# The first chunk of four routed stages is counted and placed directly behind its choice, ahead of the other work of the two engines

## What is computed

```python
for layer in (L0_ffn, L0_attn, L0_ffn, L1_ffn, L1_attn, L1_ffn, L2_ffn, L2_attn, L2_ffn, L3_ffn, L3_attn, L3_ffn):
    x = x + (0.5 if it is an ffn else 1.0) * layer(layernorm(x))

def L1_ffn(x):                      # 16 experts, at most 640 choices each
    probs = softmax(x @ router_w + router_b)
    vals, idx = top_k(probs, 2); vals = vals / (sum(vals) + 1e-9)
    oh_e = one_hot(idx.reshape(-1), 16)
    pos = (cumsum(oh_e, axis=0) * oh_e).sum(axis=1) - 1     # place among the expert's tokens
    within = pos < 640
    y = mlp_of_expert(idx, x) * vals * within               # silu(x @ wg) * (x @ wu) @ wd
    return x + mlp(x, shared weights) + sum over the two choices of y

def L2_ffn(x):                      # 8 experts, no limit
    scores = softmax(x @ gate_w.T); idx = top_k(scores + gate_b, 2)
    return sum over the two choices of scores[idx] * expert(idx, x) + expert(x, shared weights)
```

## Time and profile before

| | us |
|---|---|
| median of 3 runs | 3057.28 |
| the runs | 3051.14 to 3066.15 |
| the profiled execution | 3060.05 |
| its span, first to last instruction | 3058.6 |
| busy: PE, DVE, ACT, POOL | 2527.5, 2111.4, 1805.1, 1184.4 |
| mean granted TensorE clock | 0.908 of full speed |

### The profile page before, as it was taken

The page is one execution under the profiler, slowest core; times in us unless marked ns, Lnnn a source line. Parts: engine busy times, 40 slices in busy tenths (PEclk is TensorE's granted clock), DMA queues, the critical chain, the costliest instruction groups (busy, mean ns, idle before and its releaser), DMA issues.

```text
span 3058.6 us, 67855 instructions
## 1 busy us (share of the span) xinstructions
PE 2527.5 (83%) x25429; PEld 1999.9 (65%) x25429; DVE 2111.4 (69%) x7749; ACT 1805.1 (59%) x3508; POOL 1184.4 (39%) x1634
## 2 busy tenths in 40 slices
PE   7889988759598776669489999999999977784885
PEld 3466665447377554446479999999999865453554
DVE  6667766864377833844588888888888887336876
ACT  5344445424264432446379999999999855452553
POOL 4200003566433656565662222222222236555412
PEclk9799998879798788779799999999999998896997
DMA  9900000014110133235100000000000001441001
GB/s 238 285 13 3 3 3 1 15 60 143 59 46 3 44 116 108 90 100 170 44 24 13 1 14 13 1 13 7 7 14 1 1 1 44 132 141 30 23 3 29
DMA packets 148390, 157.20 MB, mean 51 GB/s; under 512 B 15585, under 2 KB 123746, under 8 KB 148066
## 3 DMA queue, kind: packets, MB, share of 16 engines
q1 hardware_dynamic: 119618, 78.14, 9.6%
q0 software_dynamic: 28448, 74.71, 7.7%
HBM read 77.79 MB, written 75.01 MB: 50 GB/s over the span
## 4 chain that ended last, share of the span: by engine, by line
PE 40%; DVE 10%; POOL 5%; issue 3%; DMA 1%; ACT 1%; POOLq 0%; DVEq 0%; ACTq 0%
PE banks L3244 7%; PE banks L3259 7%; PE banks L3189 3%; POOL bins L2982 3%; PE banks L3225 2%; PE banks L3198 2%; PE banks L3206 2%; PE banks L3224 2%; PE banks L3182 2%; PE banks L3020 1%; PE banks L3021 1%; PE banks L3031 1%; PE banks L3033 1%; PE banks L3022 1%; POOL results L1439 1%
## 5 line engine op out<-in xcount | busy, mean ns | idle before, releaser
L3341 POOL TENSOR_SCALAR shared_floats<-shared_floats 128x2 f32<-128x2 f32 x256 | 57.3, 224 | 658.0 <-DVE shared_floats L3332 657.8
L3259 PE MATMUL banks<-layer,shared_floats 128*128 128x128 f32 x2048 | 291.2, 275 | 0.0
L3259 PEld LDWEIGHTS banks<-layer,shared_floats 128*128 128x128 f32 x2048 | 258.8, 192 | 0.0
L3244 PE MATMUL banks<-shared_floats,layer 128*128 128x256 f32 x1024 | 245.5, 383 | 0.0
L3580 ACT ACTIVATE shared_floats<-banks,layer 128x256 f32<-128x256 f32 x512 | 210.4, 471 | 52.0 <-PE banks L3244 51.9
L3244 PEld LDWEIGHTS banks<-shared_floats,layer 128*128 128x128 f32 x1024 | 187.5, 193 | 20.8
L3343 POOL TENSOR_TENSOR shared_floats<-shared_floats,neg_half 128x2 f32<-128x2 f32 x256 | 183.2, 716 | 21.3
L1359 POOL DMA_INDIRECT results<-shared_floats,e_token_rows x160 | 155.0, 969 | 88.9 <-issue 48.2
L3353 DVE TENSOR_SCALAR shared_floats<-banks,shared_floats 128x128 f32<-128x128 f32 x512 | 185.9, 404 | 4.0 <-POOL shared_floats L3343 4.0
L244 PE MATMUL banks<-ident,xn 128*128 128x128 f32 x320 | 63.6, 332 | 140.8 <-issue 81.7
L2131 DVE TENSOR_REDUCE shared_floats<-banks 128x2 f32<-128x512 f32 (+3 forms) x256 | 110.8, 485 | 95.9 <-PE banks L1995 94.6
(11 more groups left out here) (398 smaller groups left out, 7974.0 us busy)
## 6 DMA issues: line engine op xcount, KB each, us to landing
bins<-zero SPq DMA_DIRECT2D x1, 18176.0 KB, 70.1
bins<-layer SPq DMA_DIRECT2D x16, 650.0 KB, 12.3
shared_floats<-bins SPq DMA_DIRECT2D x32, 325.0 KB, 3.7
expert_weights<-in_dram_experts SPq DMA_DIRECT2D x32, 312.0 KB, 3.0
results<-results SPq DMA_DIRECT2D x32, 256.0 KB, 3.2
layer<-in_dram_layers SPq DMA_DIRECT2D x8, 902.0 KB, 4.5
results<-zero SPq DMA_DIRECT2D x1, 4096.0 KB, 16.1
bins<-xn,f_bin_row POOLq DMA_INDIRECT x256, 2.3
```

What stands on the lines that cost most here:

```text
L3244: m = T.matmul(k.bank[5 + half][:, part], w["w1"][:, tile(n)], h1[:, :], start=True, stop=True)
L3259: m = T.matmul(to, hidden[:, n * S + t * P:n * S + (t + 1) * P], w["w2"][:, tile(n)], start=False, stop=(n == NF - 1), skip_group_check=True)
```

## The change

In `ffn1` on PE, `count(0)` goes ahead of `ln_turn(1)`. On DVE, the clearing of the carried counts goes ahead of `route(0)`; `place(0)` goes directly behind `route(0)`; `apply(1)`, which was inside `route(0)`, goes behind `place(0)`, and so do the two clearings of e_hidden1. In `ffn2` on PE, `widen` is split in its two wide matmuls and the tails (`widen_tails`), and `count(0)` goes between the two, ahead of the tails and of `logits(1)`. On DVE, `place(0)` goes directly behind `route(0)`, ahead of `statistics(2)` (in the run that has it) and of `multiply(0)`. The chunks 1 to 7 keep their order; no instruction is added or taken away; ACT, POOL and SP keep theirs. The lines of the new kernel are up to 9 higher.

```diff
 def ffn1_tensor
     logits(0)
+    count(0)
     ln_turn(k, s, 1)
-    count(0)
     for i in range(NC):
         widen(i)
 def ffn1_vector
-        if i + 1 < NC:
+        if i and i + 1 < NC:
             apply(i + 1)
         top_weights(k, n, 1e-9)
...
     v.count(V.memset(hidden[1][:, :], 0.0))
+    v.count(V.memset(carry[:, :], 0.0))
     route(0)
-    v.count(V.memset(carry[:, :], 0.0))
+    place(0)
+    apply(1)
     for n in range(2):
         v.count(V.memset(k.sb(f"e_hidden1_{n}", [P, CAPACITY])[:, :], 0.0))
-    V.wait_ge(v.sem, v.n)
     for i in range(NC):
         n = s.c0 + i
-        place(i)
+        if i:
+            place(i)
         multiply(i)
 def ffn2_tensor
         m.then_inc(k.sem("f1_gate_up"), 1)
+
+    def widen_tails(i):
+        n, xnT = s.c0 + i, k.xnT(s.t0 + i)
         if i:
             T.wait_ge(k.sem("g_product"), products_before(s) + 2 * i)
...
     widen(0)
+    count(0)
+    widen_tails(0)
     logits(1)
-    count(0)
     for i in range(NC):
         if i + 1 < NC:
             widen(i + 1)
+            widen_tails(i + 1)
         narrow(i)
 def ffn2_vector
     route(0)
+    place(0)
     if not s.early:
         statistics(2)
     for i in range(NC):
         n = s.c0 + i
         multiply(i)
-        place(i)
+        if i:
+            place(i)
```

## The result

| | before | after |
|---|---|---|
| median, 20 runs each | 3058.62 | 3064.01 |
| the runs | 3051.14 to 3073.05 | 3054.21 to 3071.44 |
| profiled execution, its span | 3060.05, 3058.6 | 3064.38, 3062.9 |
| mean granted TensorE clock | 0.908 | 0.906 |

Times are in us. The ratio of after to before is 1.002, 95% interval 1.001 to 1.0029: 6.1 us slower, 3.1 to 8.9. The single parts show more in the traces, where a stage can be measured from a fixed point.

A forecast was written before the change was run, and what follows sets the result against it. The prediction took POOL's sends to bound the routing halves, in ffn1 from the first send of chunk 1 on. Terms 3.1 + 3.1 + 1.4 - 1.7 = +5.9 gave a median of 3063, range 3051 to 3074.

The forecast's parts named there:

- Who sets the half in ffn1: ffn1: POOL's first send of chunk 1, released by DVE's row numbers, sets the end; each run +3.1.
- The early row numbers: ffn1, chunk 0: DVE's row numbers come 2.3 to 2.4 earlier, but POOL then idles about 7 before chunk 1.
- Rival A: All routing halves: the placed chunk starts the sends and their start counts; -2.3, -2.3, +1.4, -2.0, giving 3052; chance 10%.
- The late norm: ffn1, chunk 1: norm 3.4 later delays PE's transposes, wide matmuls and chunk 0's products; each run +3.1.
- The lower bound of 2.0: ffn1, each run: loss of only 2.0 instead of 3.1 if PE's clock is up earlier.
- ffn2, first run: DVE waits 1.4 for PE's count, so statistics and POOL's first send come later; +1.4, bounds 0.9 and 1.8.
- Its work is the same, so all behind it comes 1.4 later: ffn2, first run, DVE: after the 1.4 wait for the count, unchanged work delays everything behind by 1.4.
- ffn2, second run: Placing and first send 2.0 earlier, chunk 1's feed 0.3 late against its start; -1.7, bounds -2.0 and -0.6.
- The sum: Whole program: 3.1 + 3.1 + 1.4 - 1.7 = +5.9, median 3063 against 3057.28.
- Rival B: Whole program: the stages behind take up the shifts of 3 us each, leaving 3057; chance 12%.
- Rival C: ffn1: longer PE idle keeps its clock low through the half, 9 us more per run, 3081; chance 6%.
- The rule against the trace: ffn1, chunk 0 sends: trace allows 0.23 per send beside DVE's work, the skill's port rule up to 1.1 per run.

The follow-up runs named there:

- ffn1 part alone: Only the ffn1 part of the change, both runs, ffn2 as before; median 3060.45 against 3056.04 for before, ratio 1.0018.
- norm kept: The ffn1 part of the change, but the norm of chunk 1 stays inside route(0); ffn2 as before; median 3057.31, ratio 1.0006 to before.
- the last kernel: Against before: ffn1 change with PE's wide matmuls of chunk 0 ahead and norm inside route(0), ffn2 change in its second run; 3050.29 against 3055.88, ratio 0.9983.
- `ffn2` part alone: Only the ffn2 part of the change, both runs, ffn1 as before; median 3059.86 against 3056.04 for before, ratio 1.0008.
- `ffn2`'s second run alone: ffn2 part with DVE's new order in the second run only, PE's in both; ffn1 as before; 3059.1 against 3056.04, ratio 1.0006.
- kernel with the clearings ahead of `route(0)`: ffn1 change with PE's wide matmuls of chunk 0 ahead, norm inside route(0), e_hidden1 clearings ahead of it; 3182.86 against 3181.66 for before, ratio 1.0005.

## Why the prediction was right, step by step

- **Who sets the half in ffn1.** The first send of chunk 1 did. The table compares it with the last send. Each difference is against traces that have the stage as before: in the first run the mean of three (18.31 and 96.93; the clock at chunk 1 made no difference there), in the second run the mean of the two with the high clock at chunk 1 (18.59 and 94.91), or the one with the low (18.81 and 97.48).

| | first send of chunk 1 | last send |
|---|---|---|
| after, first run | 20.94, +2.6 | 99.95, +3.0 |
| ffn1 part alone, first | 19.54, +1.2 | 97.97, +1.0 |
| norm kept, first | 17.72, -0.6 | 96.73, -0.2 |
| the last kernel, first | 16.27, -2.0 | 94.78, -2.1 |
| after, second run (low clock) | 21.53, +2.7 | 99.75, +2.3 |
| ffn1 part alone, second | 21.53, +2.9 | 97.82, +2.9 |
| norm kept, second (low clock) | 18.46, -0.4 | 96.79, -0.7 |
| the last kernel, second | 16.06, -2.5 | 92.79, -2.1 |

  The two move together to 0.5. That DVE sets this send is not so in every execution. With the `ffn2` part alone, where the first run of `ffn1` is as before, the wide matmuls of chunk 0 took 2.98, and POOL's own eight sends were the limit:

```profile
599.69 1.04 POOL L1185 DMA_INDIRECT bins<-xn,f_bin_row  x1 [0.28 <-POOL xn L1181]
```

- **The early row numbers.** 2.3 to 2.4 earlier was expected, 2.53 measured (5.89 to 3.36), and it brought nothing, as POOL's new wait of 6.24 and 7.14 (predicted: 7) shows. Rival A falls.
- **The late norm.** Transposes 3.4 later were expected and came 3.17 later; wide matmuls 2.81 for 3.1; DVE's wait for ACT 3.91 for 4; products 2.67 for 3.1. The half ended 3.0 later in the first run (1.0 where the clock rose early) and 2.3 to 2.9 in the second, for 3.1. The lower bound of 2.0 named that clock as its reason, and the kernel in which it happened lost less than the bound allowed. Against the one trace with the stage as before in which the clock rose as early (2.98 for the four, last send 96.70) it lost 1.3: what was late there came partly out of time that POOL's sends took in any case.
- **ffn2, first run.** The wait for the count: 1.56 for 1.4. POOL's first send 1.47 later (9.35 behind the cast for 7.88), as expected. But 2.1 is lost at the end, where the forecast had 1.4, with 1.8 as its upper bound. The step that failed is "Its work is the same, so all behind it comes 1.4 later". It left out ACT, which the prediction weighed in the second run alone. Before, DVE's placing of 1.9 us stood between the products of chunk 0 and the choice of chunk 1, and beside it ACT worked on the products and reloaded its function table. Now the placing is ahead, and DVE reaches the sum of exponentials 0.53 before ACT is through 1.40 of activation and 1.28 of loading. The two waits, 1.56 and 0.53, make the 2.1.
- **ffn2, second run.** First send 2.1 earlier, for 2.0. The feed of chunk 1 is 0.72 late against its start (15.09 for 14.37), not 0.3: the same wait for ACT (0.64), in part made up by DVE's turning to chunk 1 earlier, and 0.44 for the down projection, which the low clock puts off. POOL stood idle for 1.10 at chunk 1, where 0.30 is usual, and -1.05 is left, against -1.7 forecast; inside the bounds of -2.0 and -0.6. In the last kernel, at the high clock, the 0.44 is not there, the feed comes at 14.45 (0.2 late against 14.26, the mean of the three with the stage as before), and -1.75 is left. So the working holds; what it left out is that PE now waits 0.90 ahead of the wide matmuls of chunk 1 and had the low clock there in four of six traces.
- **The sum.** With like clocks 3.0, 2.3 to 2.9, 2.1 and -1.05 make 6.4 to 7.0, against +5.9 forecast and 6.1 by the ratio. The terms of `ffn2` were both 0.7 too low, the first for the wait for ACT and the second for the clock, and those of `ffn1` a little too high; that the median came out at 3064 for 3063 owes something to that, and something to luck. The forecast was added to 3057.28, the median of three runs; that of 20 is 3058.62, and the two medians of 20 differ by 5.4.
- **Rival B, absorbed:** falls. PE's first transposes of expert rows, in the first run of `ffn1` of after, beside the earlier trace rows:

```profile
680.91 1.30 PE L1227 MATMUL banks<-ident,shared_floats 128*128 128x128 f32 x5 [17.45 <-DMA shared_floats<-bins]
```

  They start 5.58 behind the last send (675.33), and 5.43 behind it before (682.43 less 579.88 + 97.12): what stands behind the sends moved with them.
- **Rival C, the clock:** not seen in `ffn1`, for which it was made. In after the wide matmuls are back at 1.88 by chunk 1 in the first run. The low level at chunk 1 of the second appears without the change as well. In `ffn2` a small form of it did come, with the cost of 0.7 above.
- **The rule against the trace.** The case did not come up at chunk 0: the late norm (578.66 to 579.78) was all but over when POOL's first send began (579.64), and the second send began behind the clearings (581.19 against 581.12). The first, beside the clearings, took 1.25, as in before. Norms of later chunks do run beside sends, in the trace of before too:

```profile
591.82 1.20 DVE L214 TENSOR_SCALAR xn<-x,mean_var,rstd 128x128 f32<-128x128 f32 x4
```

```profile
592.00 1.00 POOL L1185 DMA_INDIRECT bins<-xn,f_bin_row  x1 [0.30 <-issue]
```

  The send took 1.00, where 0.96 is usual, and the norm 1.20 for 1.11. The hold-up of up to 1.1 that the prediction worked out by the rule (the Trainium skill, SBUF — State Buffer, "Who interferes with whom") does not show there. The 1.19 that the prediction went by repeats: in the first run of `ffn2` in before, all four sends that began while DVE added two SBUF tiles (L1494) took 1.19 or 1.20.

What the trace shows of ACT bears on a second page. The table load took 1.28 and began 0.03 behind the activation ahead of it (1245.21 + 1.40 to 1246.64); the exponentials followed at once. The Trainium skill, ScalarE: Activation LUTs, "What ACT_TABLE_LOAD costs", gives 1283 ns for the load, which the row confirms, and 1380 ns of draining besides, which it does not show. With the draining, by the page's figure, DVE's wait would have been 1.9 (an estimate, 0.53 + 1.38).

## What to carry to other kernels

Ask from which transfer on the consumer no longer waits; here, work that was made early for a transfer ahead of that one brought nothing. A step that looks free to move on its own engine (here a norm of 1.1 us) is paid for where another engine's queue, which is worked off in order, waits for it: look for what stands behind it there. When a block is moved out from between two steps, look for the third engine whose work it covered.

## What the runs showed beside that

- The clock of a given chunk's wide matmuls in `ffn1` differs from execution to execution of the same stage (1.88 for four of them, or 3.4 to 3.8, or between the two where the level changed midway). In the second run of `ffn1` a low level at chunk 1 costs 2.6; in the first run (3.16 in the kernel with `ffn2`'s second run alone) it costs nothing, as POOL has its root to work out there and is slower than DVE.
- In the second run of `ffn1` POOL stood idle for 1.64 or 1.65 between its first and second send of chunk 2, with nothing to wait for, in all ten traces in which it had waited ahead of the first (two of them shown), and for 0.63 to 0.68 in the four in which it had not; 0.30 is usual. The cause is open.
- On two chips the same kernels take 4% longer, with 7 to 17 late signals in each of the routing halves, whose releaser the trace cannot name. Why, is open; for a change of a few us, kernels from different chips cannot be compared behind the first of these.
- The kernel with the clearings ahead of `route(0)` was expected to save another 0.6 to 0.9 in each run of `ffn1`, and with late signals it looked worse than the one with them behind the placing (ratio 1.0005 and 0.998), although the row numbers of chunk 1 came at 14.0 to 14.2 instead of 15.3 to 17.5. Its traces show how little was left to gain: POOL's first send of chunk 1, with nothing but POOL's own work ahead of it (0.28 idle), starts at 16.08 and 15.71, against 16.27 and 16.06 in the last kernel, and the clearings stand ahead of the cast, outside these times. On a chip without late signals it was not tried.
